# Attention scores with keys on partitions in a gated cross-attention kernel

## The reference

```python
q = (layernorm(x) @ wq) -> [8, 32 heads, 56, 128];   k = (ctx @ wk), v = (ctx @ wv) -> [8, 8 heads, 1500, 128]
q, k = rope(q), rope(k)
raw  = einsum('bhqd,bhkd->bhqk', q, k) / sqrt(128)
attn = softmax(raw + mask, axis=-1)
out  = einsum('bhqk,bhkd->bhqd', attn, v) @ wo
x = x + tanh(g_xattn) * out;   x = x + tanh(g_ffn) * lora_experts(layernorm(x))
```

## Time and profile before

| | us |
|---|---|
| median of 3 runs (2006.73 to 2007.7) | 2007.14 |
| span of the profiled execution, first to last instruction | 2005.4 |
| PE busy, share | 1976.7, 99% |
| DVE busy, share | 1235.0, 62% |
| ACT busy, share | 1034.3, 52% |
| POOL busy, share | 311.6, 16% |
| one batch of attention (each of batches 2 to 7) | 224.20 |

### The profile page before, as it was taken

One profiled execution on the slowest core, in us unless ns is written; L12 is line 12 of the kernel. 1 busy time (PEld: TensorE's weight loads), 2 busy tenths in 40 slices (PEclk: granted clock), 3 DMA queues, 4 the chain that ended last, 5 costly groups with the idle time before them and its releaser, 6 DMA issues. The chain is left out here.

```text
span 2005.4 us, 32965 instructions
## 1 busy us (share of the span) xinstructions
PE 1976.7 (99%) x12404; PEld 1775.9 (89%) x12404; DVE 1235.0 (62%) x2639; ACT 1034.3 (52%) x1754; POOL 311.6 (16%) x227
## 2 busy tenths in 40 slices
PE   7999999999999999999999999999999999999998
PEld 7989889988899988998899988998899998999786
DVE  6766556666666666666666666666665666566544
ACT  6655555554545555555644555455554555455532
POOL 5511111111111111111111111111111111111200
PEclk9999999999999999999999999999999999999998
DMA  7611212111211212221111112221111112121270
GB/s 227 248 56 35 35 18 44 35 31 20 43 10 33 36 17 44 35 35 20 39 19 25 35 20 41 36 35 20 39 25 26 28 20 41 36 33 15 48 263 19
DMA packets 74904, 94.41 MB, mean 47 GB/s; under 512 B 22692, under 2 KB 49444, under 8 KB 74760
## 3 DMA queue, kind: packets, MB, share of 16 engines
q1 hardware_dynamic: 73752, 86.01, 20.4%
q10 hardware_dynamic: 1008, 6.42, 0.8%
HBM read 76.64 MB, written 15.77 MB: 46 GB/s over the span
## 5 line engine op out<-in xcount | busy, mean ns | idle before, releaser
L673 POOL TENSOR_TENSOR k_lo<-k_work,k_hi 128x500 fp32r<-128x500 f32 x192 | 244.1, 1285 | 1541.0 <-ACT k_hi L720 1513.3
L821 PE MATMUL low_banks<-wv_hi,cT_hi 128*125 128x256 f32 x1536 | 443.1, 288 | 0.0
L821 PE MATMUL low_banks<-wv_hi,cT_lo 128*125 128x256 f32 x1536 | 431.0, 281 | 0.0
L821 PE MATMUL low_banks<-wv_lo,cT_hi 128*125 128x256 f32 x1536 | 430.9, 281 | 0.0
L1027 DVE TENSOR_TENSOR pT<-t_banks,pT 125x448 fp32r<-125x448 f32 x384 | 236.0, 622 | 242.8 <-ACT pT L785 242.8
L1002 DVE CUSTOM_DVE_ANT_0 prob<-low_banks,mask_t 112x500 f32<-112x500 f32 x384 | 259.1, 678 | 178.2 <-PE low_banks L845 176.9
L785 ACT ACTIVATE pT<-t_banks 125x448 fp32r<-125x448 f32 x384 | 205.1, 543 | 309.2 <-PE t_banks L857 308.2
L760 ACT ACTIVATE prob<-prob,neg_max 112x1500 f32<-112x1500 f32 x128 | 198.6, 1552 | 289.7 <-DVE neg_max L1007 288.9
L805 PE MATMUL low_banks<-cT_hi,wk_hi 128*128 128x500 f32 x768 | 312.0, 406 | 0.0
L805 PE MATMUL low_banks<-cT_hi,wk_lo 128*128 128x500 f32 x768 | 298.6, 389 | 0.0
L805 PE MATMUL low_banks<-cT_lo,wk_hi 128*128 128x500 f32 x768 | 298.3, 388 | 0.0
(11 more groups left out here) (136 smaller groups left out, 2910.2 us busy)
## 6 DMA issues: line engine op xcount, KB each, us to landing
stage<-in_ctx_dram SPq DMA_DIRECT2D x72, 250.0 KB
attn_by_head<-attn SPq DMA_DIRECT2D x65, 112.0 KB, 1.7
wq_raw<-in_L_xattn_wq_dram SPq DMA_DIRECT2D x7, 1024.0 KB, 7.2
q_raw<-q_by_head SPq DMA_DIRECT2D x64, 112.0 KB, 4.9
inv_b<-inv_by_head SPq DMA_DIRECT2D x64, 112.0 KB, 5.1
head_rows<-in_ctx_dram SPq DMA_DIRECT2D x24, 250.0 KB
mask_t<-in_mask_BxSxS_ff_dram SPq DMA_DIRECT2D x16, 328.1 KB
stage<-in_L_xattn_wo_dram SPq DMA_DIRECT2D x4, 1024.0 KB, 7.3
```

The lines of the kernel that those rows point to most:

```text
L673: nc.gpsimd.tensor_tensor(k[1][:, c * SC:(c + 1) * SC], k_rot[:, s], f32(k[0][:, c * SC:(c + 1) * SC]), ALU.subtract).then_inc(k_lo, 1)
L821: mm = nc.tensor.matmul(sv_banks[0:ST, m % 2, t * PAIR:(t + 1) * PAIR], cT[a][:, d, tile * ST:(tile + 1) * ST], w[1][mv][:, d, g * DH:g * ...
```

## The change

Scores are computed with keys on partitions: the stationary operand is a tile of 125 keys and the moving one the 224 query rows. The 24 transposes of probabilities in a step go. The softmax then needs maxima and sums over partitions. VectorE adds the mask (`mask`, now a plain add of a turned mask) and takes elementwise maxima over the 12 key tiles (`max`, `half`); TensorE turns the result (`MT`), VectorE reduces it (`rows`), TensorE spreads it over partitions (`MB`), ScalarE copies it (`maxb`). GpSimd subtracts it from the scores (`sub`, 6), ScalarE takes the exponential (`exp`, 6) and hi (`T`), VectorE lo (`T`), now from SBUF on both sides. GpSimd adds the exponentials (`add`, 5, and `total`); TensorE turns that sum in the next step (`SUM`), and `inv` moves from the end of its own step into the next step, the step of its `norm`. The mask is turned once a batch (`B`). The tables are new, with more kinds of steps (zero, even, pre, odd, turn by group 0, 2/4, 6, 1/3/5, 7), and GpSimd has one too. The diff, cut to its core:

```diff
 PE_STEP = {
-    "even": ("K00 S0 S1 K01 K02 S2 S3 K03 K10 S4 S5 K11 K12 K13 V40 K20 T0 T1 K21 V41 K22 T2 K23 PV0 V50 T3 PV1 T4 "
-             "V51 PV2 T5 PV3 PV4 PV5"),
...
+    "even": ("S0 S1 K00 S2 S3 SUM S4 K01 S5 K02 K03 K10 K11 K12 MT K13 MB V40 V41 V50 V51 PV0 PV1 PV2 K20 K21 K22 "
+             "K23 PV3 PV4 PV5"),
...
 ACT_STEP = {
+    "even": "Q swap0 maxb swap1 exp0 T0 exp1 T1 V4 exp2 T2 V5 exp3 T3 exp4 T4 K0 exp5 T5 swap2 out K1 K2",
...
 DVE_STEP = {
+    "zero": ("mask0 mask1 max1 mask2 mask3 max2 inv max3 mask4 mask5 max4 max5 half rows cos0 sin0 rot0 cos1 Q "
+             "norm T0 sin1 rot1 T1 T2 T3 V4 V5 T4 T5 cos2 sin2 out rot2"),
+    "odd": ("mask0 mask1 max1 mask2 max2 mask3 mask4 max3 max4 inv mask5 max5 half cos0 rows sin0 rot0 Q cos1 "
+             "sin1 rot1 T0 T1 T2 V0 norm V1 T3 T4 T5 cos2 sin2 rot2 V2 V3 out"),
...
+POOL_STEP = {
+    "even": "sub0 sub1 sub2 sub3 sub4 sub5 add1 klo0 add2 add3 klo1 klo2 add4 add5 total",
...
 def scores (TensorE)
-            for n, (a, m) in enumerate(PASSES):
-                mm = nc.tensor.matmul(sv_banks[0:ROWS, i % 2, 0:SC], q[a][:, h * ROWS:(h + 1) * ROWS],
-                                      k[m][:, c * SC:(c + 1) * SC], start=(n == 0), stop=(n == len(PASSES) - 1))
+            for t in range(2):
+                tile = slice((2 * j + t) * ST, (2 * j + t + 1) * ST)
+                for n, (a, m) in enumerate(PASSES):
+                    mm = nc.tensor.matmul(t_banks[0:ST, item % 2, t * GQ:(t + 1) * GQ], k[a][:, tile], q[m][:, :],
+                                          start=(n == 0), stop=(n == len(PASSES) - 1))
...
 GpSimd
+                    nc.gpsimd.tensor_tensor(bank_weights(j), bank_weights(j), max_b[:, None, :].broadcast_to([ST, 2, GQ]),
+                                            ALU.subtract).then_inc(p_shifted, 1)
...
+                    nc.gpsimd.tensor_tensor(key_sum[:, :, :], so_far, bank_weights(j), ALU.add).then_inc(p_added, 1)
...
 VectorE
+            so_far = bank_weights(0) if j == 1 else key_max[:, :, :]
+            nc.vector.tensor_tensor(key_max[:, :, :], so_far, bank_weights(j), ALU.max).then_inc(max_steps, 1)
...
+        def normalise(n):
+
+            if n:
+                dve.wait_ge(o_free, n)
+            dve.wait_ge(inv_loaded, 16 * (n + 1))
+            nc.vector.tensor_tensor(o_sum[:, :], o_sum[:, :], inv_b[:, :], ALU.mult).then_inc(attn_ready, 1)
...
 SyncE, in each step
+        def spread_inv(b, g):
+
+            wait_apart(sp, inv_ready, b * HKV + (g + 1), sp_passed)
+            with nc.allow_non_contiguous_dma("224 numbers"):
+                sp.dma_start(inv_dram[(g - 1) % HKV].rearrange("h r -> r h"), inv_sum[:, :]).then_inc(inv_stored, 16)
+            wait_apart(sp, inv_stored, b * (16 * HKV) + 16 * (g + 1), sp_passed)
+            sp.dma_start(inv_b[:, :], inv_dram[(g - 1) % HKV:(g - 1) % HKV + 1].rearrange("g h r -> g (h r)").broadcast_to(
+                [P, GQ])).then_inc(inv_loaded, 16)
```

More of the change, by code:

```diff
@@ L90 @@
 DVE_STEP = {
[8 rows of a table removed]
[14 rows of a table added]
+             "out lastinv O1"),
+    "first": "C2 C3 V0 C4 C5 C6 V1 C7 cos0 C8 sin0 C9 rot0 C10 C11 cos1 sin1 rot1 Q B0 B1 cos2 sin2 V2 rot2 V3",
+}
+POOL_STEP = {
[7 rows of a table added]
 }
 def step_kind(g, last):
-    return ("last" if last else "turn") if g == HKV - 1 else ("odd" if g % 2 else "even")
-def act_kind(g, last):
-    return "pre" if last and g == HKV - 2 else step_kind(g, last)
+    if last and g >= HKV - 2:
+        return "last" if g == HKV - 1 else "pre_last"
+    return ("zero", "odd", "even", "odd", "even", "odd", "pre", "turn")[g]
 def tasks(order):
@@ L114, in tasks @@
         digits = word[len(what):]
-        numbers = tuple(int(x) for x in digits) if what in ("K", "V") else (int(digits),) if digits else (0,)
+        numbers = tuple(int(x) for x in digits) if what in ("K", "V", "O") else (int(digits),) if digits else (0,)
         yield what, numbers
 def t_fills(table, kind):
-    return [(what, n) for what, (n, *_) in tasks(table[kind]) if what in ("C", "T")]
+    return [("S" if what == "mask" else what, n) for what, (n, *_) in tasks(table[kind]) if what in ("C", "S", "B", "mask")]
 def t_place(kind, what, n):
     fills = t_fills(PE_STEP, kind)
-    assert fills == t_fills(ACT_STEP, kind) == t_fills(DVE_STEP, kind)
-    assert t_fills(ACT_STEP, "pre") == t_fills(ACT_STEP, "even")
+    assert fills == t_fills(DVE_STEP, kind)
     return fills.index((what, n))
@@ L139, in k_item, with t_item, v_item, next_pair @@
     return b * K_ITEMS + g * NC + c
[L142 to L159, removed]
+def t_item(b, g, what, n, last=False):
+    return b * T_ITEMS + (T_FIRST + g * PT + t_place(step_kind(g, last), what, n))
+def v_item(pair, m):
+    return pair * VT + m
+def next_pair(step):
+    return (step + step % 2) // 2
 def wait_apart(eng, sem, value, passed):
@@ L849, in transposes, with mask_transposes @@
-        def transposes(b, g, s, j, last):
-            pe.wait_ge(t_free, t_item(b, g, j, last) + 1)
-            if j == 0:
-                pe.wait_ge(p_ready, b * (HKV * HALVES) + (g + 1) * HALVES)
+        def mask_transposes(b, item, s, part):
+            pe.wait_ge(t_free, item + 1)
+            pe.wait_ge(shared.mask_loaded, b * 32 + 32)
+            for i in range(MASK_TILES):
+                mm = nc.tensor.transpose(t_banks[0:ST, s, i * 2 * SQ:(i + 1) * 2 * SQ],
+                                         shared.mask_rows[:, part * MASK_TILES + i, :], ident[0:2 * SQ, 0:2 * SQ])
+            mm.then_inc(t_ready, 1)
@@ L907, in step @@
                 if what == "C":
-                    c_transposes(b + 1, c_item(b, *n), t_bank, *n)
-                if what == "T":
-                    transposes(b, g, t_bank, *n, last)
+                    item = t_item(b, g, "C", *n)
+                    c_transposes(b + 1, item, item % 2, *n)
+                if what == "B":
+                    item = t_item(b, g, "B", *n)
+                    mask_transposes(b + 1, item, item % 2, *n)
+                if what == "SUM" and step_n:
+                    turn_sums(step_n - 1)
@@ new lines, in normalise @@
+        def normalise(n):
+            if n:
+                dve.wait_ge(o_free, n)
+            dve.wait_ge(inv_loaded, 16 * (n + 1))
+            nc.vector.tensor_tensor(o_sum[:, :], o_sum[:, :], inv_b[:, :], ALU.mult).then_inc(attn_ready, 1)
+        def step(b, g, last):
+            n, kn = b * HKV + g, k_item(b, g + 1)
+            for what, (j, *_) in tasks(DVE_STEP[step_kind(g, last)]):
+                s = ((g + 1) * NC + j) % 2
+                if what == "mask":
+                    add_mask(b, g, j, last)
+                if what == "max":
+                    max_part(b, g, j, last)
+                if what == "half":
+                    max_half(n)
+                if what == "rows":
+                    max_rows(n)
+                if what == "inv" and n:
+                    invert_sums(n - 1)
+                if what == "lastinv":
+                    invert_sums(n)
@@ L1178, in _ @@
         with sp.Fori(1, pairs - 1) as i:
[L1179 removed]
+            for u in range(2):
+                output_load(sp, shared, wo, attn_dram, i, u, sp_passed)
         for t in range(NTT):
```

438 lines of the change are left out of this document (249 added, 189 removed), and 58 rows, old and new, of tables (ACT_STEP, DVE_STEP, PE_STEP, POOL_STEP).

## The result

The changed kernel takes 2429.62 us (median of 4 runs, 2422.83 to 2438.28) against 2007.42 us for the kernel before on the same chip: ratio 1.210, 95% interval 1.207 to 1.214. The forecast was 2165, range 1950 to 2290. Slower was right; 158 us were forecast and 422 measured.

What follows compares the result with a forecast made beforehand. TensorE, busy in 99% of the span, was taken as the bound. Per batch 208.2 work + 21.6 `inv_b` wait + 12 GpSimd beside VectorE + 2 clock = 243.8 us against 224.2, giving 2165 us, range 1950 to 2290.

Steps and rivals of the forecast that it cites:

- TensorE's work: On TensorE: transposes removed, narrower scores and small transposes added, taking a batch from 224.2 to 208.2 us.
- wait for `inv_b`: First value product waits for the reciprocals' DMA round trip: 6.2 us in even and pre steps, 21.6 us a batch.
- GpSimd beside VectorE: Instructions of both engines reading SBUF exclude each other, delaying VectorE: 12 us a batch, bounds 0 to 17.
- the walk: Going down the engines' queues by kind of step with alternate turns: 247 us a batch against 230, so 17 us.
- the softmax chain itself: From MB's result through copy, `sub`, `exp`, hi and lo: some 3.5 us, covered by four value parts, cost 0.
- The clock: TensorE's clock drops after three 6 us waits a batch: 2 us a batch, bounds 0 to 4.4.
- Rival 3: VectorE is the bound, with alternation at full price and all clock drops: 2225 us, up to 2290; chance 0.20.
- Total at SUM: TensorE's wait at SUM, the transposes of the summed exponentials, for GpSimd's total: put at nothing.
- The listed signs of rightness: PE near 90%, 6 us first-PV waits, two-SBUF DVE instructions 0.9 us or more, POOL over 1.15, low clock, odd steps losing little.

Runs made afterwards that it cites:

- norm_late_light: Changed kernel with the multiplication by inv_b later in VectorE's queue and GpSimd's subtractions and additions on 8 of 224 columns: 1962.91 us, ratio 0.978.
- light: Changed kernel with GpSimd's subtractions and additions on 8 of the 224 columns: 2159.98 us, ratio 1.075.
- the small program: Separate program with only 125 x 448 instructions on GpSimd and VectorE, alone and together: VectorE's 12 from SBUF take 16.76 us beside GpSimd instead of 6.51.
- write_only: Changed kernel with each GpSimd subtraction and addition on 8 of 224 columns, followed by two fills that hardly read SBUF: 2290.36 us.
- keep_warm: Changed kernel with idle matmuls (44, 44, 24, 16 in even, pre, zero, odd steps) ahead of the first value product: 2364.83 us, ratio 1.178.
- norm_late_warm: Changed kernel with the multiplication by inv_b later and idle matmuls (24, 24, 16, 12) ahead of the first value product: 2278.66 us, ratio 1.135.
- norm_late: Changed kernel with the multiplication by inv_b moved later in VectorE's queue in zero, even, pre and turn steps: 2295.82 us, ratio 1.144.

## Why the prediction failed in size

Per batch, from differences of medians by 8:

| | forecast | measured | from |
|---|---|---|---|
| TensorE's work, with what still waits | 208.2 (time 1879) | +10.5 | norm_late_light 1963 against 1879 |
| wait for `inv_b`, with its clock | 21.6 + 2 | 24.6 | light less norm_late_light, 197 us |
| GpSimd beside VectorE, with its clock | 12 | 33.7 | changed kernel less light, 270 us |

The three are 265 us more than forecast, which is the whole miss: 84, 8 and 174 us. The split depends on the order: with the wait taken off first it is 134 us for the wait and 333 for GpSimd's share.

The same by TensorE's own time, from the windows of a batch. The row of light is

```profile
848.31:1090.25 241.94, 219.45 (x1448) 199.83 (x1447) 177.37 (x302) 119.69 (x229) 65.83 (x120) 0.95 0.15 27
```

| us a batch | idle | busy |
|---|---|---|
| forecast | 33.6 (21.6 + 12) | 210.2 (208.2 + 2) |
| changed kernel | 46.5 | 230.0 |
| light | 22.5 | 219.5 |
| norm_late_light | 6.4 | 212.7 |

**The failed step is the term of GpSimd beside VectorE**: 12 us with bounds 0 to 17, measured 33.7. The mechanism was right (taking turns, whole remainders, instructions that read a bank untouched), and so was the price of a meeting (0.9 against 0.93 us). VectorE did not even lose as much as the upper bound had it: between light and the changed kernel its 302 instructions of a batch get 38.1 us longer (177.4 to 215.5), 4.8 a step, where 9.3 were counted for an even one. What failed is the part of it that reaches the time. The prediction let VectorE's slack and the wait for `inv_b` take up most of it; measured, TensorE is idle 24.0 us longer and, at its lower clock, busy 10.5 us longer.

Where it falls shows in the steps of batch 3, from first score to first score. Against light, the three odd steps are 14.5 us longer (32.9 or 33.0 each against 28.0 to 28.3, with 2.5 us of wait for the first lo half), where the walk had 4.5; the turn is 6.5 longer (46.6), where it had 2.5. The two even steps, where VectorE waits for `inv_b` anyway, are 3.9 longer, where it had 5.0. Even the walk with all turns at full price ended at 247 us a batch; 276.5 lies beyond it. (The walk's own steps without collisions add up to 228.3 and not 230, so its upper bound was 18.7 and not 17; that changes nothing here.)

Two things were missing in the term. It counted only VectorE's delay, but GpSimd is delayed as well (0.39 us a meeting in the small program, means of 1.38 and 1.41 us in the kernel against 1.13 for one alone), and it stands in the chain. And GpSimd's own length was free ("the softmax chain itself: cost 0"): write_only leaves at most 130 of the 270 us to it, most of them in TensorE's waits for k_lo and at SUM, which the fills themselves lengthened. How the 270 us part into turns (139 at least) and length is not shown further. That each station of the chain adds its delay is argued from these waits.

**The clock** was forecast at 2 us a batch from one wait in the last step; this is the second step that failed. It is 1.2 GHz for 391 us in all, and in the windows the same 1448 matmuls are busy 17.3 us longer than in norm_late_light (230.0 against 212.7). In the first table these us stand in the lower two rows, 6.8 and 10.5. The forecast counted on three waits a batch; in batch 3 TensorE waited before the first value product in all eight steps, 2.3 to 6.5 us. keep_warm showed 65 us, 8 a batch, that can be had back by keeping TensorE busy; in norm_late_warm it was 2 a batch. How much more it costs with no filler at all stays open: the idle matmuls cost time of their own.

**TensorE's work** was nearly right: 212.7 us busy in norm_late_light against 208.2. The 10.5 us are mostly 6.4 us idle (3.4 of them scores that wait for k_lo) and the turn step (39.6 us against a count of 33.5, of which 3.8 idle).

**The wait for `inv_b`** was right in place. In light, where little else delays, the first value product waits 6.0 and 5.4 us in the even steps (6.2 forecast), 4.3 in pre (6.2), 0.9 in zero (2.0) and 1.1 in the turn (1). The total, 24.6 against 23.6 us, is partly luck: TensorE is idle 16.1 us longer than in norm_late_light and not 21.6, and busy 6.8 us longer by its clock and not 2. In the changed kernel the waits in even and pre steps are 5.9 to 6.5 us. norm_late gave back 134 us and not 197: while VectorE waited, GpSimd had worked freely, and this cover went with the wait (pT from 1152 to 1424 ns).

**Rival 3** (VectorE the bound, 2225 to 2290) came nearest. VectorE was busy in 78% of a batch (215.5 of 276.5), and so not the bound of the whole; in odd steps it was busy in 90%, and in norm_late in 90% of the batch. Total at SUM, put at nothing, was 19.4 us in 18 waits in all. The listed signs of rightness all appeared (waits at the first value product, pT over 0.9, mask at 0.61, GpSimd above 1.15), except two: PE is at 83% and not near 90, and odd steps lose 3.4 us against the walk's 29.5, and 4.9 against TensorE's 28.0, and not little.

## What to carry to other kernels

Before work moves to an idle engine, look where its operands are and who waits for the result: here VectorE with both operands in SBUF and GpSimd reading SBUF took turns, and both got longer. Slack that is an average over steps does not take such delays up: look in each kind of step whether the delayed instruction has something behind it that TensorE needs. When a DMA round trip moves into a step, measure it from its last input to its first user, and put at least that much other work between them. And where new waits of some us appear ahead of matmuls, count the slow clock behind each of them as a cost of its own, as far as TensorE is what the step waits for.

## What was not expected of the hardware

- A meeting costs both sides: 125 x 448 on VectorE 0.54 alone and 1.47 us beside GpSimd, on GpSimd 1.09 and 1.48. A pair needs 1.47 us, less than the sum of 1.63.
- Mixed in turn on VectorE beside GpSimd, instructions from a bank kept 0.61 us and those from SBUF took 1.01, one of each in 1.47 us: as long as one from SBUF alone in its turn, so the one from a bank came free.
- Waits of 2.3 to 6.5 us before the first value products and a slow clock came together: 391 us at 1.2 GHz. Idle matmuls, more work, made the kernel 65 us faster; where VectorE was busy in 90% of a batch they were worth 17 us.
- 8.4 us a step of GpSimd additions from SBUF, behind the last k_lo, cost the kernel before nothing measurable (ratio 1.0006). VectorE's busy time rose by only 1.6 us a batch.
